# The row maximum of the attention scores taken as a minimum of negated scores, without the 128x4 step between

## The reference, cut to what matters

```
q = q * 64 ** -0.5
sim = q @ k.T                      # 256 x 256, causal mask: sim = -big above the diagonal
attn = softmax(sim, axis=-1)       # exp(sim - rowmax(sim)) / rowsum
out  = attn @ v
```

## Time and profile before

| | |
|---|---|
| median of 3 runs | 622.34 us (621.33 to 622.46) |
| span of the profiled execution | 622.0 us |
| TensorE busy | 578.0 us, 93% |
| VectorE busy | 525.0 us, 84% |
| ScalarE busy | 390.3 us, 63% |
| GpSimd busy | 361.7 us, 58% |
| 128x4 operation L653, in all | 38.2 us, 64 instructions |
| granted TensorE clock | full, but for the first part of the opening |

### The profile page before, as it was taken

The page is one execution under the profiler, slowest core; times in us unless marked ns, Lnnn a source line. Parts: engine busy times, 40 slices in busy tenths (PEclk is TensorE's granted clock), DMA queues, the critical chain, the costliest instruction groups (busy, mean ns, idle before and its releaser), DMA issues.

```text
span 622.0 us, 13348 instructions
## 1 busy us (share of the span) xinstructions
PE 578.0 (93%) x4230; PEld 532.1 (86%) x4230; DVE 525.0 (84%) x1473; ACT 390.3 (63%) x1021; POOL 361.7 (58%) x322
## 2 busy tenths in 40 slices
PE   4889888999999999999999999999999999878997
PEld 2877777989989899889989899898998899767887
DVE  4779987999789987999879996999879998799642
ACT  3545981589627892389725895378824897279711
POOL 0747764666638574575746665485745756475532
PEclk8999999999999999999999999999999999999999
DMA  6510000000000000000000000000000000000000
GB/s 208 173 47 1 1 18 1 3 0 20 1 17 0 0 17 17 0 0 0 17 17 0 0 17 0 17 0 0 17 17 0 0 0 0 17 1 2 1 18 19
DMA packets 7194, 10.60 MB, mean 17 GB/s; under 512 B 641, under 2 KB 5121, under 8 KB 7169
## 3 DMA queue, kind: packets, MB, share of 16 engines
q1 hardware_dynamic: 7168, 10.29, 5.3%
HBM read 8.19 MB, written 2.10 MB: 17 GB/s over the span
## 4 chain that ended last, share of the span: by engine, by line
PE 41%; DVE 27%; issue 19%; ACT 6%; POOL 5%; DMA 1%; DVEq 1%; POOLq 0%; SPq 0%; ACTq 0%
PE bank L787 28%; PE bank L874 5%; DVE q_t L596 5%; DVE probs L646 5%; PE bank L796 5%; DVE rope_s L620 3%; ACT probs L425 3%; PE bank L852 3%; DVE hid L683 2%; DVE o_sums L667 1%; POOL hid_lo L310 1%; DVE stats L532 1%; DVE rope_c L616 1%; DVE xn L575 1%; POOL o_t_lo L320 1%
## 5 line engine op out<-in xcount | busy, mean ns | idle before, releaser
L301 POOL TENSOR_TENSOR probs<-probs,inv_sum 128x512 f32<-128x512 f32 (+1 forms) x64 | 93.9, 1467 | 49.3 <-DVE inv_sum L660 49.3
L425 ACT ACTIVATE probs<-probs,neg_max 128x128 f32<-128x128 f32 (+1 forms) x256 | 113.1, 447 | 6.3 <-DVE neg_max L653 5.4
L310 POOL TENSOR_TENSOR hid_lo<-hid,hid_hi 128x512 fp32r<-128x512 f32 x64 | 84.0, 1312 | 32.6 <-ACT hid_hi L460 32.6
L787 PE MATMUL bank<-xf_t_hi,gate_hi 128*128 128x256 f32 x256 | 75.6, 295 | 10.5 <-issue 5.8
L787 PE MATMUL bank<-down_hi,hid_hi 128*128 128x256 f32 x256 | 73.9, 289 | 1.0 <-POOL hid_lo L310 1.0
L787 PE MATMUL bank<-xf_t_hi,up_hi 128*128 128x256 f32 x256 | 74.4, 291 | 0.0
L787 PE MATMUL bank<-down_hi,hid_lo 128*128 128x256 f32 x256 | 72.5, 283 | 0.0
L787 PE MATMUL bank<-down_lo,hid_hi 128*128 128x256 f32 x256 | 72.4, 283 | 0.0
L787 PE MATMUL bank<-xf_t_hi,gate_lo 128*128 128x256 f32 x256 | 72.1, 282 | 0.0
L787 PE MATMUL bank<-xf_t_lo,gate_hi 128*128 128x256 f32 x256 | 72.1, 281 | 0.0
L787 PE MATMUL bank<-xf_t_hi,up_lo 128*128 128x256 f32 x256 | 71.9, 281 | 0.0
(11 more groups left out here) (106 smaller groups left out, 1900.9 us busy)
## 6 DMA issues: line engine op xcount, KB each, us to landing
out<-y_out SPq DMA_DIRECT2D x8, 256.0 KB, 2.2
x_in<-in_x SPq DMA_DIRECT2D x7, 256.0 KB, 2.8
probs<-in_w_qkv SPq DMA_DIRECT2D x4, 384.0 KB, 3.5
probs<-in_w_gate SPq DMA_DIRECT2D x2, 512.0 KB, 7.2
probs<-in_w_up SPq DMA_DIRECT2D x2, 512.0 KB, 8.8
probs<-in_w_down SPq DMA_DIRECT2D x2, 512.0 KB, 5.1
probs<-in_w_out SPq DMA_DIRECT2D x2, 512.0 KB, 5.4
x<-in_x SPq DMA_DIRECT2D x1, 256.0 KB, 2.7
```

The costliest lines, as they stand in the source:

```text
L301: nc.gpsimd.tensor_tensor(part, part, inv_sum[:, slot].unsqueeze(2).broadcast_to([P, GROUP, keys]), ALU.mult).then_inc(p_done, 1)
L310: nc.gpsimd.tensor_tensor(hid_lo[:, slot].rearrange("p c n -> p (c n)"), hid[:, slot], hid_hi[:, slot].rearrange("p c n -> p (c n)").bitca ...
L425: last = nc.scalar.activation(part, part, ACT.Exp, bias=neg_max[:, slot, g:g + 1], scale=DH ** -0.5, accum_out=row_sum[:, slot, g:g + 1])
L787: last = nc.tensor.matmul(dst, a[x], b[y], start=start and i == 0, stop=stop and i == 2, skip_group_check=shared)
```

## The change

VectorE's pass now multiplies (scores + mask) by -1/8 as it writes and takes the row minimum, straight into `neg_max`: min(-s/8) = -max(s)/8. The exponential reads these negated scaled scores with scale -1. The 128x4 operation, VectorE's wait for its own writes in front of it, the tile `row_max` and the semaphore `s_max` are gone. ScalarE now waits for `s_used`, raised once by each pair: for the first pair ahead of the first exponential, for the second pair ahead of the third.

```diff
-        row_max = sb("row_max", [P, 4, GROUP])
         neg_max = sb("neg_max", [P, 4, GROUP])
...
             def exps():
                 slot, keys = c["S"] % 4, P * key_blocks(c["S"] % GROUPS)
-                act.wait_ge(s_max, turn.at(s_max, c["S"] + 1))
                 for g in range(GROUP):
                     part = probs[:, slot, g, 0:keys]
+                    if g % 2 == 0:
+                        act.wait_ge(s_used, turn.at(s_used, 2 * c["S"] + g // 2 + 1))
                     last = nc.scalar.activation(part, part, ACT.Exp, bias=neg_max[:, slot, g:g + 1],
-                                                scale=DH ** -0.5, accum_out=row_sum[:, slot, g:g + 1])
+                                                scale=-1.0, accum_out=row_sum[:, slot, g:g + 1])
                 last.then_inc(e_done, 1)
                 c["S"] += 1
...
                     last = nc.vector.tensor_tensor_reduce(
                         part, bank[S_BANKS[pair]][:, g % 2 * SEQ:g % 2 * SEQ + keys],
-                        mask_sb[:, SEQ - keys:SEQ] if second_tile else part, 1.0, -3.4e38, ALU.add, ALU.max,
-                        row_max[:, slot, g:g + 1])
+                        mask_sb[:, SEQ - keys:SEQ] if second_tile else part, -DH ** -0.5, 3.4e38, ALU.add, ALU.min,
+                        neg_max[:, slot, g:g + 1])
                 last.then_inc(s_used, 1)
-                if pair:
-                    dve.wait_ge(s_used, turn.at(s_used, 2 * c["S"] + 2))
-                    nc.vector.tensor_scalar(neg_max[:, slot], row_max[:, slot], -DH ** -0.5, None, ALU.mult
-                                            ).then_inc(s_max, 1)
-                    c["S"] += 1
+                c["S"] += pair
```

More of the change, by code:

```diff
@@ L172, in build @@
         low_copied, low_masked = (sig(n, 2 * KV_HEADS) for n in ("low_copied", "low_masked"))
-        s_max, e_done, r_done, p_done = (sig(n, GROUPS) for n in ("s_max", "e_done", "r_done", "p_done"))
+        e_done, r_done, p_done = (sig(n, GROUPS) for n in ("e_done", "r_done", "p_done"))
         o_ready, o_small, o_sum = (sig(n, JOBS["V"]) for n in ("o_ready", "o_small", "o_sum"))
```

## The result

The changed kernel takes 605.91 us (605.04 to 607.31, four runs) against 622.18 (621.33 to 622.46, four runs) of the kernel before, a ratio of 0.9726 [0.9701, 0.9751] (0.9738 between the medians). A second comparison, six runs against eleven on another chip, gave 0.9706 [0.9677, 0.9734]. Against the 622.34 us shown at the start the two ratios make it 604.0 to 605.3 us: faster, as forecast, but by more than the range allowed: 610.0 was forecast, and the range began at 605.5.

What follows compares the result with a forecast made beforehand. Bound: TensorE, with holes made by VectorE behind its 128x4 operation. Loop 11.3 + opening 0.4 + ending 0.9 = 12.6 us off 622.0: 609.4, as a median 609.7, said as 610; range 605.5 to 617.5.

Steps and rivals of the forecast that it cites:

- The three holes: TensorE idle ahead of k's transposes (0.97), gate product (0.62), group 1's value product (0.3): all close, 1.89 us a turn.
- The margins of 0.15 and 0.2: Time to spare in closing the loop's holes at k's transposes (0.15 us) and the gate product (0.2 to 0.3).
- The cause of the 597 ns: VectorE's 128x4 SBUF-to-SBUF operation, 597 ns each, waits out whatever GpSimd is doing, through a shared port pair.
- Behind it TensorE is dense and the rest of VectorE's saving is worth nothing.: Loop turn behind group 1's value product: no further gain, so the loop gives 6 x 1.89 = 11.3 us.
- Opening and ending: Ahead of and behind the loop: gains of 0.4 us (0 to 1.5) and 0.9 us (0.3 to 2).
- The median against the profiled execution: Whole kernel: the median of the runs lies 0.3 us above the profiled 622.0, turning 609.4 into 609.7.
- the minimum form: VectorE's passes: minimum for maximum costs 0 (bounds 0 and 0.28 us a pass); as a rival, 628 us, chance 0.03.
- The rows of `xn` in mid-turn: VectorE, ahead of the first hole: moved earlier they meet GpSimd's copies of k, losing 0.3 us (0 to 0.9).
- VectorE's busy time: Sign over the whole kernel: it falls by about 38 us, to 487.
- More closes than I count: Rival: passes and exponentials start earlier everywhere, opening and ending give 3 or 4 us more; 604 to 607, chance 0.10.
- No hole stayed partly open: Rival in the loop: something else is next late and a hole stays partly open; 613 to 616, chance 0.23.
- the saving was not hidden: Rival: other engines make TensorE's holes, so VectorE would just wait longer; 621 to 622, chance 0.05.

Runs made afterwards that it cites:

- e1: Changed kernel with VectorE's wait for its own writes and an unread 128x4 multiplication put back behind the second pair of all 64 groups: 622.27 us.
- e2: Changed kernel with VectorE's wait for its own writes and an unread 128x4 to 128x1 maximum reduction behind each second pair: 608.94 us.
- e8: Kernel before, all waits kept, with the 128x4 step made a negating reduction, the 1/8 moved into the pass and exponential scale 1: 608.80 us.
- e6: Changed kernel with the wait and unread 128x4 multiplication put back for groups 3 to 7 of the six loop turns only: 611.09 us.
- e13: Changed kernel with the wait and unread 128x4 multiplication put back for group 4 of the six loop turns only: 609.77 us.
- e7: Changed kernel with the wait and unread 128x4 multiplication put back outside the loop only, in the opening and the ending: 607.61 us.
- e4: Changed kernel, but ScalarE waits for both pairs ahead of the first exponential: 605.84 us.
- e3: Changed kernel with only VectorE's wait for its own writes put back behind the second pair, no instruction behind it: 608.21 us.
- e9: Changed kernel with VectorE's two rows of xn for the next sequence written one step earlier, ahead of the second rope product: 605.29 us.
- e12: Changed kernel where GpSimd holds its second sum of q in a turn until VectorE has written the two rows of xn: 602.08 us.

## Why the prediction was right, and where it was not

**The three holes.** Right, and to a hundredth: 0.96, 0.62 and 0.30 against 0.97, 0.62 and 0.30. That each closes rested on start times of VectorE. Laid on the clock of before (by the 7.3 us between the two timelines ahead of the first hole), the pass on group 2 starts at 264.45 + 7.30 = 271.75, where 271.7 was forecast; the low part of q comes 1.05 us earlier, against 1.1; the low part of x starts at 275.05, against 275.0; ScalarE's high part at 274.2, so it ends at 274.8, against 274.9. The margins of 0.15 and 0.2 were real and held.

**The cause of the 597 ns.** Right. e1 brings it back in an instruction without a reader, e2 and e8 remove it with a reduction. The fixed price by the Trainium skill's page VectorE: DVE Perf Modes (section on the TRN2 errata), an estimated 65 ns, would by itself have given about 621. It lies far below the 128x4 operation's mean, and below its shortest in e1 too, 169 ns; the same section of the Trainium skill says that the 58 cycles are too few and that it measured about 150.

**"Behind it TensorE is dense and the rest of VectorE's saving is worth nothing."** This is the step that failed: it put the second half of the turn at nothing, and the runs show 0.42 us a turn there, with 0.24 more behind the three holes. I had looked for places where a row of TensorE carried an idle bracket of 0.3 or more. What I left out is of two kinds. The step behind a wait is long too: 0.22 us instead of 0.12 at 277.57 in the kernel before; the three of them make 0.24 a turn. And TensorE waited for VectorE at three more places of the second half (286.44, 291.26, 294.69), 0.17, 0.10 and 0.09, where the rows of its products show no idle time; with 0.06 between them they make 0.42 a turn. Together 0.66 of the measured 2.57; six turns, 4.0 us, the larger part of what the forecast lacked. e6 and e13 show that the waits are VectorE's: with the filler back in these groups they come back at the same places. With 2.57 for 1.89 the sum would have been 15.4 + 1.3 = 16.7 us in place of 12.6, and the forecast 605.6.

**Opening and ending.** Mis-sized too, though less: 0.4 and 0.9 us were forecast, 0.75 and 1.28 measured between the two traces, and e7 puts back 1.4 and 1.2. Both terms were low, the two together by 0.7 to 1.2.

**The median against the profiled execution.** I put the median 0.3 above the span. The timed runs lie 1.7 to 1.8 above the span of the same run, so the execution profiled before stands for a run of about 623.8 us, 1.4 slower than the median. The forecast is still the median less the sum (622.34 - 12.6 = 609.7), so this cost it nothing; but it is why the two spans differ by 18.7 us and the kernels by about 17.

**Costed at nothing, and nothing it was:** the minimum form (417 and 286 ns, 413 and 284 before), ScalarE's early start on the first pair (e4), the scale of the exponential (a mean of 394 and 503 ns, 393 and 501 before). The rows of `xn` in mid-turn grew as a pair from 0.81 us (268.98 in the kernel before) to 0.90 (261.59 after), less than the 0.3 I took off.

**VectorE's busy time** was to fall to 487 and fell to 494.3. A blocked instruction overlaps the next one by 0.08 to 0.09 us in the records (271.79 + 1.11 against 272.82), and the busy time counts such a stretch once: 64 times 0.09 is 5 of the 7 us. The rest is slightly longer passes and reads, and rows of `xn` beside GpSimd.

**The rivals.** "More closes than I count" is what happened (604 to 607, given 0.10), but not where I put it: I had named the ends, where 0.7 us more came, and most was in the loop, 4.0 us. No hole stayed partly open, the saving was not hidden, and the minimum form cost nothing.

## What to carry to other kernels

A small elementwise operation from SBUF to SBUF on VectorE can cost what is left of GpSimd's running instruction, as those at 266.68 and 271.79 did, so look at the spread of its durations (169 to 1302 ns for four elements a partition), not at its size; when it can't go, a reducing or accumulating form of it, or one wait on GpSimd's side, takes most of the cost away. When you count what a faster engine gives its consumer, line up the starts of the consumer's instructions over a whole period and sum every excess over the bare step, tenths too, and look at the weight loads' waits beside the products': the large idle brackets held only three quarters of it here.

## What the hardware showed beyond this

- A wait of VectorE for its own last write has a price without any instruction behind it: in e3 the next pass starts 0.31 us behind the accumulator read, 0.07 without the wait. It cost 0.37 us a turn, most of the 0.47 that wait and reduction cost together in e2.
- Between two rows of one VectorE loop GpSimd gets in if it becomes ready during the first: in e9 the pair takes 1.70 us, with GpSimd starting 0.24 after it; in e12, where GpSimd's next instruction is held back, 0.76. And there the pair's first 0.29 us lie beside GpSimd's running sum at no visible cost (first row 0.43 us), which the blocks of 1.1 us at the earlier trace rows would not have let expect. It is so in the kernel after too: the first row (242.88) starts 0.28 ahead of the end of a sum and takes 0.44, and the whole loss is in the second, 1.38. Why is open.
- A product of TensorE that had to wait is followed by its successor after 0.22 us in place of 0.12 (277.57 and 277.79 against 268.64 and 268.75), so this hole costs 0.1 us more than the distance ahead of it; behind the transposes of k it is 0.05.
- In a custom two-input pass with PSUM input the minimum costs as much as the maximum, to 4 ns, for 128 and for 256 keys.
